# Where a per-channel factor is undone in the self-attention: from the copy of the head output to the softmax denominator

## The reference

```
x = x + attn(layernorm(x), w_q, w_k, w_v, w_o)        # one head, head dim 128
x = x + xattn(layernorm(x), ctx, mask, W, b)          # relu projections, masked softmax, times ctx
x = x + ffn(layernorm(x), w_gate, w_up, w_down)       # quantised activations, ternary weights
```

```
q, k, v = x @ w_q, x @ w_k, x @ w_v
A = softmax(q @ k.T / sqrt(128))
y = ((A @ v) * head_dim_mask) @ w_o
```

## Time and profile before

| | |
|---|---|
| median of 3 runs | 361.74 us (361.67 to 361.78) |
| the profiled execution | 361.78 us |
| its span, first to last instruction | 359.9 us |
| granted TensorE clock, mean | 1.00 |
| ACT busy | 313.7 us (87%) |
| POOL busy | 293.1 us (81%) |

### The profile page before, as it was taken

How to read it: one execution, slowest core, us unless ns; L and a number is a source line. 1 busy time by engine, 2 the same in 40 slices (tenths; PEclk the granted TensorE clock), 3 DMA queues, 4 the chain that set the end, 5 groups by cost and what they waited for, 6 DMA issues and landing times.

```text
span 359.9 us, 7050 instructions
## 1 busy us (share of the span) xinstructions
PE 349.1 (97%) x1922; PEld 258.2 (72%) x1948; DVE 312.9 (87%) x916; ACT 313.7 (87%) x583; POOL 293.1 (81%) x421
## 2 busy tenths in 40 slices
PE   8999899999999999999999999999899999999996
PEld 6476578876887767776786678777587768667655
DVE  3769949948899899998899889999899889899994
ACT  2598999999899977999889986999679988987995
POOL 1657779369899998899968998899877997895886
PEclk9999999999999999999999999999999999999999
DMA  7986731725206644557275568238434633312353
GB/s 264 425 229 221 189 90 31 140 67 197 54 14 139 143 146 122 103 124 172 92 176 120 112 180 240 47 81 170 90 58 94 157 55 79 73 32 44 61 163 131
DMA packets 84695, 46.09 MB, mean 128 GB/s; under 512 B 76208, under 2 KB 77872, under 8 KB 84272
## 3 DMA queue, kind: packets, MB, share of 16 engines
q1 hardware_dynamic: 84656, 45.64, 50.3%
HBM read 23.07 MB, written 4.21 MB: 76 GB/s over the span
## 4 chain that ended last, share of the span: by engine, by line
PE 71%; DVE 8%; ACT 8%; POOL 5%; issue 5%; DMA 1%; SPq 1%; ACTq 0%; DVEq 0%; POOLq 0%
PE b_bank L1135 7%; PE b_bank L1136 7%; PE b_bank L1137 7%; PE d_bank L1372 5%; PE g_bank L1352 5%; PE a_bank L1135 5%; PE u_bank L1352 5%; PE a_bank L1137 5%; PE a_bank L1136 5%; PE b_bank L1280 2%; PE a_bank L1217 2%; POOL xp_lo L706 2%; PE b_bank L1251 1%; PE e_bank L1135 1%; PE e_bank L1137 1%
## 5 line engine op out<-in xcount | busy, mean ns | idle before, releaser
L753 POOL TENSOR_TENSOR c_work<-c_work 128x512 f32<-128x512 f32 x48 | 61.4, 1290 | 6.5 <-DVE c_work L1624 4.6
L1023 ACT ACTIVATE c_work<-g_bank,c_tanh_scale 128x512 f32<-128x512 f32 x52 | 36.1, 693 | 4.2 <-PE g_bank L1352 2.4
L1135 PE MATMUL b_bank<-ctx_hi,b_pT_hi 128*128 128x256 f32 x128 | 39.1, 306 | 0.2 <-DVE b_nmax L1600 0.2
L1624 DVE SCALAR_TENSOR_TENSOR c_work<-c_work,g_bank 128x512 f32<-128x512 f32 x50 | 33.9, 677 | 5.1 <-ACT c_work L1023 4.8
L1136 PE MATMUL b_bank<-ctx_lo,b_pT_hi 128*128 128x256 f32 x128 | 36.1, 282 | 0.0
L1137 PE MATMUL b_bank<-ctx_hi,b_pT_lo 128*128 128x256 f32 x128 | 36.1, 282 | 0.0
L800 POOL TENSOR_SCALAR c_work<-c_work,h_q 128x1024 f32<-128x1024 f32 x28 | 31.7, 1133 | 5.1 <-DVE h_q L1658 5.0
L1026 ACT ACTIVATE c_work<-u_bank 128x512 f32<-128x512 f32 x48 | 28.9, 602 | 5.4 <-PE u_bank L1352 5.0
L1352 PE MATMUL g_bank<-gateT,xqT 128*128 128x512 bf16 x98 | 30.5, 381 | 1.5 <-ACT xqT L998 0.5
L1352 PE MATMUL u_bank<-upT,xqT 128*128 128x512 bf16 x101 | 31.1, 381 | 0.8 <-DMA xqT<-xq 0.2
L1651 DVE TENSOR_REDUCE h_max<-c_work 128x1 f32<-128x1024 f32 x26 | 31.4, 1207 | 0.2 <-issue 0.2
(11 more groups left out here) (357 smaller groups left out, 1202.0 us busy)
## 6 DMA issues: line engine op xcount, KB each, us to landing
ctx_raw<-in_ctx SPq DMA_DIRECT2D x8, 512.0 KB, 5.0
x_all<-in_x SPq DMA_DIRECT2D x7, 512.0 KB, 4.0
a_xT_raw<-in_x_t SPq DMA_DIRECT2D x7, 512.0 KB, 4.4
ctxT_raw<-in_ctx_t SPq DMA_DIRECT2D x7, 512.0 KB, 4.5
out<-x_all SPq DMA_DIRECT2D x7, 512.0 KB, 2.9
r_bc<-r_rows SPq DMA_DIRECT2D x7, 256.0 KB, 3.6
c_work<-in_w_gate SPq DMA_DIRECT2D x1, 1024.0 KB, 9.7
c_work<-in_w_up SPq DMA_DIRECT2D x1, 1024.0 KB, 11.7
```

Of the source, the lines that this page charges most:

```text
L753: pool.tensor_tensor(h[:, t % 2, half * HALF:(half + 1) * HALF], th[:, j % 2, :], up[:, j % 2, :], ALU.mult).then_inc(hs, 1)
L1023: act.activation(gate_tile(j, n), gu_bank("g", j, n), ACT.Silu if (n, j) in SILU else ACT.Tanh, scale=c_tanh_scale[:, j // 2:j // 2 + 1]). ...
L1135: pe.matmul(dst, l_hi, r_hi, start=first, stop=False)
L1624: dve.scalar_tensor_tensor(gate_tile(j, n), gate_tile(j, n), 1.0, gu_bank("g", j, n), ALU.add, ALU.mult).then_inc(gates, 1)
```

## The change

The factor `v_range` leaves the copy of H on ACT, which becomes the plain copy of L898 for all sequences. Instead a new 128x4 tile `a_den` holds `a_sum` times `v_scale`, made by a DVE instruction in the step inv for n > 0; DVE then waits for its own result (semaphore `a_dens`), and the reciprocal reads `a_den`. As 1 / (sum x v_scale) = v_range / sum, the same number reaches x. The values in `hT` and in the PSUM banks of Y are larger by 1 / `v_range` in between. The additional wait for `v_steps` at n = 1 on ACT goes, and so does the DVE branch that is never run.

```diff
+        a_den = sb("a_den", [P, T], F32)
...
+        v16_loaded, p16_loaded, a_dens = sem("v16_loaded"), sem("p16_loaded"), sem("a_dens")
...
@@ a_hi, on ACT
-                elif n > 0 and step == "H":
-                    if n == 1:
-                        act.wait_ge(v_steps, 2)
-                    act.activation(dst[step], src[:, :], ACT.Copy, scale=v_range[:, :]).then_inc(a_his, 1)
                 else:
                     act.activation(dst[step], src[:, :], ACT.Copy).then_inc(a_his, 1)
...
@@ a_part, on DVE
-                        if n > 0 and step == "H":
-                            last = dve.scalar_tensor_tensor(lo, src[:, :], v_range[:, :], f32(hi), ALU.mult, ALU.subtract)
-                        else:
-                            last = dve.tensor_tensor(lo, src[:, :], f32(hi), ALU.subtract)
+                        last = dve.tensor_tensor(lo, src[:, :], f32(hi), ALU.subtract)
...
@@ step, on DVE
                     if n > 0:
                         dve.wait_ge(a_added, 2 * n)
-                    dve.reciprocal(a_inv[:, :], a_sum[:, :]).then_inc(a_invs, 1)
+                        dve.tensor_scalar(a_den[:, :], a_sum[:, :], v_scale[:, :], None, ALU.mult).then_inc(a_dens, 1)
+                        dve.wait_ge(a_dens, n)
+                    dve.reciprocal(a_inv[:, :], a_sum[:, :] if n == 0 else a_den[:, :]).then_inc(a_invs, 1)
```

More of the change, by code:

```diff
@@ L422, in decoder_layer @@
         v_abs, v_sums, v_steps = sem("v_abs"), sem("v_sums"), sem("v_steps")
-        v16_loaded, p16_loaded = sem("v16_loaded"), sem("p16_loaded")
+        v16_loaded, p16_loaded, a_dens = sem("v16_loaded"), sem("p16_loaded"), sem("a_dens")
         a_filled, a_his, a_los = sem("a_filled"), sem("a_his"), sem("a_los")
```

## The result

The change made the kernel slower: 365.28 us median against 362.24 us, both over ten runs; ratio 1.0065, 95% interval 1.0037 to 1.0095. That is some 2.4 us by the ratio and 3.0 us by the medians, and by the interval between 1.3 and 3.4. The forecast was 361.7 us, within 361.2 to 362.4, and no change. Two things about the measure. The runs of one kernel lie further apart than the three I had seen: before reached from 361.4 to 364.6 us, after from 362.8 to 366.0. And the profiled execution after is faster than all ten, 362.53 us with a span of 360.7, only 0.8 us over the one before; so the trace alone doesn't show the whole loss.

A forecast was written before the change was run, and what follows sets the result against it. PE's order of matmuls was taken as the bound (busy 97% of the span, 71% of the chain). 0 from ACT and 0 from DVE left the median of 361.74 us: forecast 361.7 us, range 361.2 to 362.4.

The forecast's parts named there:

- ACT's copy: Seven copies of H on ACT, each 0.09 us shorter, 0.63 us at most; PE not reached, so 0 gained.
- The wait at n = 1: ACT's additional wait for `v_steps`, removed by the change; claimed satisfied long before, so its removal changes nothing.
- DVE's pair: New multiplication plus waiting reciprocal on DVE, seven times; priced at 0.25 us each, 0.13 to 0.31, 1.75 us in all.
- The gaps behind it, n by n: DVE's idle gaps after each new pair, 0.29 to 3.39 us, claimed to absorb the 0.25 us shift everywhere: 0.
- Rival 2: DVE's shift handed on at n = 4, 5 and 7: 362.5 us for three places, 362.0 for one; chance 0.16.
- The sign "if the waits of PE for transfers change their length": On PE, in the profile after: changed lengths of its waits for transfers would show the forecast wrong; no size given.
- The Trainium skill's free semaphore: On DVE: a semaphore in a chain costs nothing extra, so the pair costs 0.13 us, 0.9 us in all; not adopted.

The follow-up runs named there:

- ACT's half: Changed kernel without the a_den instruction and its wait, factor left out of the result; against the kernel before 363.25 us, ratio 1.0025; again 363.87 us, 1.0024.
- the second profile: Profile from the rerun of the changed kernel with no edit; that run measured 365.14 us, ratio 1.0074 against the kernel before.
- the program of its own: Separate program without the decoder layer: small DVE instructions with POOL idle, then busy; the 128x4 multiplication took 0.21 to 0.26 us idle, 0.32 to 1.26 us busy.
- DVE's half: Changed kernel with the factor back in ACT's copy of H, a_den made and waited for but reciprocal reading a_sum; 364.55 us, ratio 1.0068 against the kernel before.

## Why the prediction was wrong

- *ACT's copy, 0.09 us each, no gain:* right as far as the runs can tell. 597 ns after; and the version that takes this saving and adds 0.4 us once (factor in the weights) lies at 0.9996.
- *The wait at n = 1 "had been satisfied long before; nothing":* wrong by 0.30 us. Without it ACT stands idle 0.30 us before one instruction and PE comes 0.30 us later (41.05 against 40.75); with it back, neither. The wait was satisfied, as said, but taking it out was not free. The two timings of ACT's half (1.0025 and 1.0024) would be 0.9 us; what lies beyond the 0.30 us is not explained, and the kernel before against itself was off by 0.8 us.
- *DVE's pair, 0.24 us from a 128x1 pair, 0.31 at most:* this is the step that failed. I took the price of a small instruction from its size and its operands, 0.25 us a place; measured from a_den to the reciprocal it was 1.13, 0.96, 1.31 and 1.12 us at n = 1, 3, 4 and 6, and 2.27 us at n = 3 in the second profile. The pair does cost about that at n = 2, 5 and 7 (0.23, 0.26 and 0.28 us from a_den to the reciprocal), and it did with POOL idle in the program of its own. But the 128x4 form also waits for POOL's 128x512 instructions, up to two of them, and the 128x1 form from which I priced it does not. The bound of 0.31 us was no bound, and the range did not allow for that. The trace before held one DVE instruction nearer in form, L1665: 128x512, from SBUF to SBUF, with a factor from a tile, at 353.7 and 354.1. It took 0.49 us both times with no long POOL instruction already running, so it could not have shown the wait either. I missed it, and took a 128x1 form as "just what the new pair is".
- *The gaps behind it, n by n:* sound as a method. n = 1 and 6 took up waits of 1.1 us (3.39 and 1.26 us of gap), as far as the profiles tell: with both, DVE's half still has 84.65 us in the third column. n = 4 with its 0.29 us did not: 1.27 us of wait came out as 1.1 us of lost time. At n = 3, with 0.48 us, the 0.93 us left no mark on PE and the 2.23 us did.
- *Rival 2, the shift on DVE handed on, named n = 4, 5 and 7.* That DVE's queue hands its delay on, slower, is what happened, at n = 3 and 4. The mechanism is not the rival's: there the gaps moved along because their releasers came late, here the wait was larger than the gap (1.27 against 0.29 us). n = 5 and 7, which it named, had short a_den. Its 362.5 us was for three places of 0.25; two at 1.1 make 2.2 us, against 2.4 by the ratio and 3.2 by the ratio of the version with these two alone.
- *The sign "if the waits of PE for transfers change their length"* came true as well: in the second profile PE waits 1.86 us for the softmax transposes at n = 5 and 6, before 1.04 us. ACT's half, without a_den, shows 1.77 and 1.26 us, and DVE's half 0.35 us, so this part of the loss is not shown to come from the wait for POOL.
- *The Trainium skill's free semaphore, 0.13 us each:* not what the runs show. Even with POOL out of the way the pair took 0.23 us and more. In the version with four 128x1 multiplications these start 0.09 to 0.13 us apart, and the reciprocal, which waits, starts 0.23 to 0.25 us behind the last.

What is settled: the form of the instruction (1.0012 against 1.0074 side by side), the place (1.0087 against 1.0030), the wait for POOL (by the program of its own). In the profiles it accounts for 1.1 us at n = 4 and, when it goes over two instructions, for 1.0 to 1.1 us more at n = 3. The rest isn't settled to the last tenth: the stretch from n = 4 to 6 moves by up to 1.2 us between profiles of one kernel and 2.2 us between all of them, how often a_den at n = 3 draws the long wait is known from four profiles only (two long, two short), and whether the changed kernel draws the bad end more often than the kernel before was not separated. Nor is it shown why one wait fewer on ACT costs 0.30 us; that it hangs on the number of instructions in its queue fits three cases (one fewer, the same, more), but what in the chip depends on it was not tried.

## What to carry to other kernels

A small VectorE instruction has two prices, its own and the rest of what GpSimd is doing. Before a form that the trace doesn't show is priced from its neighbour, look whether it differs in having more than one column, in SBUF for both source and result, or in two SBUF inputs, and read GpSimd's timeline at each place where it will stand: at n = 1, 3, 4 and 6 GpSimd was already in a 1.3 us TENSOR_TENSOR of 128x512, at n = 2 and 7 between shorter ones, at n = 5 in one of 128x2. Here a 128x4 reciprocal, a 128x1 multiplication and a 128x4 one from PSUM passed it.

## What the runs showed of the hardware

- A waiting DVE instruction isn't always let in when POOL's ends. Where POOL's next one follows at once it was held for both (2.23 and 2.24 us) in two profiles, and got in between them after 0.93 and 0.95 us in two others.
- Not every GpSimd instruction held it: inside c_rstd (128x2, 0.70 us) the 128x4 multiplication took its 0.22 us.
- The four 128x1 multiplications took 0.54 to 0.58 us where one 128x4 with nothing in its way takes 0.20 to 0.25; still the cheaper choice beside a busy POOL.
- Taking a satisfied wait out of ACT's queue put 0.30 us of idle time on ACT at a place some 90 us later, in all seven profiles of kernels without it that put nothing else into ACT's queue.
